# Eight gelu tiles of a pair: the high parts of tiles 0 to 4 move from VectorE's casts to ScalarE's copies

## What is computed

```python
h = patches @ W + b, joined with table[x_txt]
h = h + attn0(layernorm(h))
# the feed-forward part of layer 0
def ternary_linear(x, w):
    w_t = sign(w) * (abs(w) > 0.5 * mean(abs(w)))
    return (x / (rms(x) + eps)) @ w_t.T
g = gelu(ternary_linear(layernorm(h), w_up))      # [tokens, 1024]
h = h + ternary_linear(g, w_down)                 # the rms of g is divided out
h = h + recurrent_attn1(layernorm(h))             # part_b
h = h + experts1(layernorm(h))                    # part_c
```

## Time and profile before

| | |
|---|---|
| three runs | 1054.66, 1056.12, 1063.71 us |
| the profiled execution | 1061.87 us |
| its span, first to last instruction | 1060.0 us |
| granted TensorE clock, mean | 0.945 |
| TensorE busy | 945.3 us (89%) |
| VectorE busy | 793.9 us (75%) |
| ScalarE busy | 590.9 us (56%) |
| GpSimd busy | 544.2 us (51%) |

### The profile page before, as it was taken

The page is one execution under the profiler, slowest core; times in us unless marked ns, Lnnn a source line. Parts: engine busy times, 40 slices in busy tenths (PEclk is TensorE's granted clock), DMA queues, the critical chain, the costliest instruction groups (busy, mean ns, idle before and its releaser), DMA issues. The chain is left out here.

```text
span 1060.0 us, 19336 instructions
## 1 busy us (share of the span) xinstructions
PE 945.3 (89%) x5800; PEld 840.6 (79%) x5800; DVE 793.9 (75%) x2393; ACT 590.9 (56%) x1175; POOL 544.2 (51%) x652
## 2 busy tenths in 40 slices
PE   2279999999999999875989999999998999973998
PEld 2269999999999999874568888888887888863787
DVE  2647777777777777663368999999997899972676
ACT  2036666666666666552546666777665677621342
POOL 2126666666666665453424555545544455432564
PEclk9589999999999999897989999999999999965899
DMA  3201311111111114002299999999999999982310
GB/s 128 80 21 31 41 41 40 40 40 42 45 45 42 42 42 160 16 16 76 29 123 145 155 155 153 155 154 154 155 145 135 150 156 148 139 104 91 120 60 21
DMA packets 134814, 96.32 MB, mean 91 GB/s; under 512 B 11208, under 2 KB 129104, under 8 KB 134096
## 3 DMA queue, kind: packets, MB, share of 16 engines
q1 hardware_dynamic: 133200, 91.20, 56.5%
q0 software_dynamic: 1536, 4.20, 1.4%
HBM read 31.92 MB, written 13.11 MB: 42 GB/s over the span
## 5 line engine op out<-in xcount | busy, mean ns | idle before, releaser
L300 POOL TENSOR_TENSOR gelu_lo<-gelu_out,gelu_hi 128x384 fp32r<-128x384 f32 x128 | 152.0, 1213 | 34.4 <-DVE gelu_hi L492 32.4
L898 POOL TENSOR_TENSOR B_decayed_u<-B_scan_in 128x512 f32<-128x512 f32 x48 | 62.1, 1294 | 89.6 <-DMA B_scan_in<-B_stage 77.9
L615 PE MATMUL psA<-x2T_hi,ternary_up 128*128 128x384 f32 x256 | 94.1, 368 | 10.6 <-DVE residual L595 10.4
L662 PE MATMUL psA<-ternary_down,gelu_hi 128*128 128x256 f32 x384 | 98.3, 293 | 5.0 <-POOL gelu_lo L300 4.1
L662 PE MATMUL psA<-ternary_down,gelu_lo 128*128 128x256 f32 x384 | 94.6, 284 | 0.0
L615 PE MATMUL psA<-x2T_lo,ternary_up 128*128 128x384 f32 x256 | 87.7, 343 | 0.0
L886 POOL TENSOR_TENSOR B_y<-B_scan_in,B_states 128x512 f32<-128x512 f32 x48 | 62.0, 1292 | 45.4 <-ACT B_states L957 45.4
L1134 PE MATMUL psB<-Win_hi,B_x_hi 128*128 128x512 f32 x192 | 83.6, 435 | 0.0
L1146 PEld LDWEIGHTS psB<-B_partial_dots,B_minus_same_batch 128*128 128x128 f32 x384 | 67.2, 196 | 20.3 <-DVE B_partial_dots L1030 9.0
L662 PEld LDWEIGHTS psA<-ternary_down,gelu_hi 128*128 128x128 f32 x384 | 73.3, 191 | 9.7 <-POOL gelu_lo L300 8.6
L1046 DVE SCALAR_TENSOR_TENSOR psB<-B_decayed_u,psB 128x128 f32<-128x128 f32 x192 | 68.0, 354 | 14.4 <-PE psB L1146 14.3
(11 more groups left out here) (248 smaller groups left out, 3345.5 us busy)
## 6 DMA issues: line engine op xcount, KB each, us to landing
B_scan_in<-B_stage SPq DMA_DIRECT2D x192, 256.0 KB, 7.9
patches<-in_patches SPq DMA_DIRECT2D x16, 384.0 KB, 3.2
B_residual<-layer_out SPq DMA_DIRECT2D x48, 128.0 KB, 5.0
out_dram<-B_residual SPq DMA_DIRECT2D x48, 128.0 KB, 4.7
C_raw<-in_experts SPq DMA_DIRECT2D x8, 768.0 KB, 4.2
layer_out<-residual SPq DMA_DIRECT2D x32, 128.0 KB, 1.8
layer_out<-residual SPq DMA_DIRECT2D x32, 64.0 KB, 2.0
weight_stage<-in_upT SPq DMA_DIRECT2D x1, 1024.0 KB, 6.0
```

Source lines behind the costliest of these rows:

```text
L300: nc.gpsimd.tensor_tensor(act_l[:, k, :], act[:, k % DEEP, :], act_h[:, k, :].bitcast(F32), ALU.subtract).then_inc(s["ffn_lo"], 1)
L615: last = nc.tensor.matmul(out, a, b, start=(n == 0), stop=(n == len(terms) - 1))
L662: last = nc.tensor.matmul(ps[:, 6 + k // 2, (k % 2) * D:(k % 2 + 1) * D], x[:, c, k * P:(k + 1) * P], dn_w[:, c, :], start=(c == 0 and x i ...
L898: nc.gpsimd.tensor_tensor(lu[:, j % 2], ring[:, j % R_RING, :, LAM, :], ring[:, j % R_RING, :, U, :], ALU.mult).then_inc(s["lu"], 1)
```

## The change

`hi_scalar` names all eight tiles in place of 5, 6 and 7. So ScalarE makes the high part of every gelu tile with a Copy that stands behind the square of the tile before (for tile 0 there is no square, and the Copy stands right behind its own gelu), and VectorE makes none.

```diff
         lo_vector = ()
-        hi_scalar = (5, 6, 7)
+        hi_scalar = tuple(range(FC))
         lo_pool = [k for k in range(FC) if k not in lo_vector]
```

## The result

Over 20 runs of each kernel in turn, the changed kernel took 1069.53 us in the median and the kernel before 1062.74 us. The ratio is 1.0065, with a 95% interval from 1.0043 to 1.0087: 6.9 us slower (4.6 to 9.2). The forecast was +8.3 us, and slower by less than 1%. The profiled execution of the changed kernel has a span of 1063.0 us and a mean granted clock of 0.95.

The account below looks back on a forecast made before the run. TensorE was taken to bound the stage, through waits without slack. 14 pairs at 0.61 us (+8.5) and -0.2 in pair 15 made +8.3 us, so 1056.1 became 1064.4 us, range 1058 to 1071.

Parts of the forecast that it names:

- The copies ahead of `v_hi`: Two added copies in ScalarE's queue delay v_hi, gelu 2 and up 4 by 0.61 us a pair, 8.5 us over 14 pairs.
- The Trainium skill's budget for an ACTIVATE: Price of a ScalarE copy, 0.62 us for 384 columns; it would give 0.87 us a pair, but the sum used the trace.
- Hidden, by 0.3 us: On ScalarE, xT_hi gets 1.84 us more in front of it, with 2.11 us free, so it is not late.
- Nothing that TensorE waits for stood only behind a cast. Worth 0: Taking VectorE's 5 casts a pair, 80 in all, out of its queue gains TensorE nothing.
- the 0.2 us wait for the last low part stays: TensorE's 0.2 us wait at down 0 stays, since ScalarE's copy of tile 7 releases that low part and moves with TensorE.
- a gap at `t` in place of that at `up` 4: Sign of being wrong: TensorE's gap at up 5, pv or t instead, meaning a margin of 0.3 us was misjudged.
- -0.2 us: Pair 15, with no pipeline around it: ScalarE sets the pace, 1.20 us a tile, and the last low part ends slightly earlier.
- Copies without overlap: Rival: ScalarE's copies overlap less, up to 1.09 us a pair, +15.3 us, 1071.4 us; chance 0.20 for over 1%.
- The delay is taken up: Rival: TensorE's later waits for the last low part and x_normed shrink, leaving 0.15 us a pair, +2, 1058 us; chance 0.13.
- A fall of the clock in the regular pairs: Rival: the new TensorE gap brings the 1.2 GHz level for some 3 us a pair, +29, 1085 us; chance 0.04.
- Faster: Rival: relief of VectorE and GpSimd removes TensorE's two waits, with no delay at up 4: -6.4, 1049.7 us; chance 0.03.

Follow-up runs that it names:

- e7: The changed kernel with add 2 moved behind x_split, so VectorE takes xT_lo before it: a pair of 26.32 us, ratio 1.0037 to the kernel before.
- e5: The changed kernel with the transposes pT moved ahead of up 0 and up 1: a pair of 25.86 us, ratio 0.9958 to the kernel before.
- e10: The kernel before, with all eight copies on ScalarE in pair 15 only: pair 15 took 20.63 us against 22.46, ratio 0.9982.
- e3: The changed kernel with gelu 0, gelu 1 and their copies ahead of probT_hi in ScalarE's queue: a pair of 25.70 us, ratio 1.0011 to the kernel before.
- e6: The kernel before, with the transposes pT moved ahead of up 0 and up 1: a pair of 25.14 us, ratio 0.9907.
- e9: e5 with GpSimd waiting for x_normed before the low part of tile 2: a pair of 25.17 us, ratio 0.9895 to the kernel before.
- e11: e6 with all eight copies on ScalarE in pair 15 only: a pair of 25.13 us, pair 15 in 20.64, ratio 0.9886 to the kernel before.
- e1: The kernel before, with the copies of tiles 0 and 1 also on ScalarE: a pair of 26.34 us, ratio 1.0090.
- e4: The kernel before, with the copy of tile 0 alone also moved to ScalarE: a pair of 25.93 us, ratio 1.0046.

## Why the prediction was right, and where it was not

*What bounds.* Right: TensorE is paced by waits that have no slack, and the wait that grew is that of `up` 4 for gelu 2, the one named. I had written 25.65 us for a pair; over 13 pairs it is 25.75.

*The copies ahead of `v_hi`.* Right in mechanism and nearly in size. "`v_hi` is late by 0.61 us": 0.69 was measured (2.21 less 1.52). The missing 0.08 is mostly the wait of the copy for its own gelu, taken at 0.05 from VectorE and measured at 0.10 on ScalarE; another 0.02 is rounding in the sum, since its own steps put `v_hi` at 216.40, which is 0.63 behind 215.77. The gap before `up` 4 grew by 0.60, from 0.13 to 0.73.

The Trainium skill's budget for an ACTIVATE ("ScalarE: Activation LUTs", section "Rules for kernel authors") is given there for an ACTIVATE whose bias is a pointer operand of one value per partition. The gelus, squares and copies here are issued without a bias (L371, L362, L380), so the prediction applied it where it does not bear, and the trace shows it: they are recorded at 0.47 to 0.55 us and, but for the copy of tile 0, follow each other by 0.37 to 0.43, not by the 0.62 that the budget makes for 384 columns, and a pair grew by 0.56 us and not by 0.87. The exponentials of L393 do have such a bias. For their 256 columns the budget makes 0.51 us, an estimate from the page, and the trace of the kernel before has 0.49 to 0.51.

*"Hidden, by 0.3 us"* for `xT_hi` was right: it still waits 0.27 us on average for TensorE. `v_lo` was in time as well.

*VectorE and GpSimd* were wrong twice. "Nothing that TensorE waits for stood only behind a cast. Worth 0": true of the casts, but the adds and `x_normed` that stay in the queue got slower (1.86 us for three `x_normed` instead of 1.06, and 2.65 us for two adds), and made `xT_lo` and `t` 0.33 us late. I had let the new low parts fall where they would and had not asked which VectorE work they would meet. And "the 0.2 us wait for the last low part stays" was wrong for that reason: TensorE comes to it 0.33 us later, finds the low part there, and finds `x_normed` of the second norm there too. By the rows: +0.60 at `up` 4, +0.33 at `t`, -0.19 and -0.16 at the two others, +0.58; the rhythm says +0.56. e7 shows that the last three terms cancel: without the gap at `t`, the other two waits come back and the pair is as long. The prediction had named a gap at `t` in place of that at `up` 4 as a sign of being wrong. It came beside that one, and not by a misjudged margin on ScalarE but by VectorE's queue. So the size per pair was near its mark partly because two things that were left out took each other up, and that was luck.

The rule of the Trainium skill that GpSimd shares its SBUF interfaces with VectorE, with contention from VectorE instructions in a 2-port mode or with two SBUF inputs ("GPSIMD Engine Reference", section "Key points"), agrees with the trace for the adds: they have two SBUF inputs, and took 0.56 us each in that place before and 2.65 for two after. The three `x_normed` were held up as well, 2.81 us in e5 against 1.06; whether they run in a 2-port mode no run here shows. I read the rule as relief for GpSimd alone. In e5 the contention costs VectorE, and TensorE behind it, 0.7 us a pair.

*The last pairs.* "-0.2 us" for pair 15 and 0 for pair 14 were the terms most off: -2.65 and -0.78 in the profiles. The chain that I priced, gelu 0 to the end of the last low part, went from 11.76 (471.38 to 483.14) to 11.30 us (478.77 to 490.07), -0.46. The rest came with the clock, which I had left out of this place: 0.67 us between the h2 before and gelu 0, where the granted clock was 0.66 before and 0.98 after, and 1.52 us behind the last low part, where it was 0.62 and 1.00. Pair 14 is scatter, by e10. The last h2 is thus 5.4 us later in the profiles, where the prediction had 8.5 - 0.2 = +8.3. The runs say +6.9, and their interval, 4.6 to 9.2, holds both; how often the last pair has the low clock in them is not known.

*The rivals.* Copies without overlap (+15) did not occur. "The delay is taken up" was half there: the two waits that it named did vanish, but were refilled by the gap at `t`. A fall of the clock in the regular pairs did not occur: 1.00 from 100 to 400 us. Faster did not occur; what it needed was no queue ahead of `v_hi`, and e3, which has that, is level with the kernel before (1.0011).

## What to carry to other kernels

An engine that is free by its sum can still have no room at one place of its queue. Count what stands between the instruction whose input comes last and the one that the bottleneck waits for, and put extra work into the idle stretch before it: e3 has the same eight copies as the changed kernel and is 0.6 us a pair shorter. When work leaves an engine that takes turns with another, ask what the other will now do earlier, and beside which instruction. The largest gap of a pair was a third place: with five transposes moved into it, e6, e9 and e11 are about 1% faster than the kernel before.

## What the runs showed that I had not expected

An added wait made a kernel faster (e9: 25.86 to 25.17 us a pair), since it keeps a `gelu_lo` of GpSimd from starting just ahead of `x_normed` on VectorE. Single `x_normed` instructions of 256 columns took 0.40 to 0.43 us in the kernel before and had a median of 1.10 us in e5, so a tensor_scalar between two SBUF tiles, and not only adds and casts, waits for a running `gelu_lo`. And TensorE ran largely at the 1.2 GHz level behind the last low part in three of the four kernels that make three casts or more in the last pair (before, e1, e4, not e6), and in none of the nine with two or none, in one profiled execution of each. What decides it is not shown.
